# A mixture-of-experts layer on one core: the closing sum split over ScalarE, VectorE and GpSimd, with the first gated rows in PSUM

## What is computed

```python
x = x + attention(layernorm(x))
n = layernorm(x)
route_w = softmax(n @ Wr + br)                  # 8 experts
routed  = route_w * mask_of_the_top_2
routed  = routed / routed.sum(-1)               # two gates for each token
h       = relu(n @ W1[e] + b1[e])               # each expert, 128 -> 512
y[e]    = h @ W2[e] + b2[e]                     # 512 -> 128
out     = x + sum_e routed[e] * y[e]
```

## Time and profile before

| | |
|---|---|
| time before, median of 3 runs | 353.44 us (353.34 to 354.66) |
| the profiled execution: its own time | 355.26 us |
| its span | 353.5 us |
| busy in the span: PE, DVE, ACT, POOL | 294.8, 285.2, 222.9, 249.3 us |
| last scatter issued by GpSimd | 329.50 us |
| first of the eight loads issued | 332.47 us |
| first scaling and first sum | 336.27 and 336.28 us |
| last sum ends | 350.77 us |

### The profile page before, as it was taken

The page is one execution under the profiler, slowest core; times in us unless marked ns, Lnnn a source line. Parts: engine busy times, 40 slices in busy tenths (PEclk is TensorE's granted clock), DMA queues, the critical chain, the costliest instruction groups (busy, mean ns, idle before and its releaser), DMA issues.

```text
span 353.5 us, 7837 instructions
## 1 busy us (share of the span) xinstructions
PE 294.8 (83%) x2237; PEld 209.9 (59%) x2237; DVE 285.2 (81%) x623; ACT 222.9 (63%) x644; POOL 249.3 (71%) x251
## 2 busy tenths in 40 slices
PE   5899999989979999799867699999999999997000
PEld 5677845545545555555424477778888888886000
DVE  5888899999886999999899549997777777772196
ACT  2688711488878745245434886768888888882092
POOL 4639995454979998898777477777777777777300
PEclk9899999999999999899969589999999999997555
DMA  8990000000000000001111266525655454411397
GB/s 227 351 289 19 2 0 0 0 4 0 1 0 0 2 23 26 23 23 53 56 45 52 48 98 109 100 71 96 103 100 107 107 100 108 105 58 52 106 401 236
DMA packets 50026, 29.16 MB, mean 82 GB/s; under 512 B 34993, under 2 KB 44639, under 8 KB 49986
## 3 DMA queue, kind: packets, MB, share of 16 engines
q1 hardware_dynamic: 45142, 19.02, 22.4%
q0 software_dynamic: 4544, 9.38, 9.5%
q10 hardware_dynamic: 300, 0.27, 0.2%
HBM read 10.87 MB, written 12.67 MB: 67 GB/s over the span
## 4 chain that ended last, share of the span: by engine, by line
PE 41%; DVE 29%; issue 10%; ACT 9%; POOL 8%; DMA 2%; POOLq 0%; ACTq 0%; DVEq 0%; SPq 0%
PE ps L1260 9%; POOL y_rows L554 7%; PE ps L1259 5%; DVE nd L914 4%; DVE work L903 4%; PE ps L1233 3%; PE ps L1421 3%; PE ps L1423 2%; PE ps L1422 2%; DVE rows L930 2%; PE ps L1440 2%; PE ps L1441 2%; PE ps L1445 2%; DVE x L1194 2%; DVE wraw L1145 2%
## 5 line engine op out<-in xcount | busy, mean ns | idle before, releaser
L554 POOL DMA_INDIRECT y_rows<-kvt,yid x78 | 74.7, 958 | 23.8 <-issue 21.3
L520 POOL DMA_INDIRECT x_rows<-rows,pos_i x64 | 62.4, 975 | 21.7 <-issue 17.8
L722 ACT ACTIVATE ps<-ps,b1s 128x256 f32<-128x256 f32 x156 | 60.4, 451 | 16.3 <-PE ps L1423 14.1
L1145 DVE TENSOR_TENSOR wraw<-ps,wraw 128x1024 f16<-128x1024 f32 x39 | 47.7, 1224 | 21.1 <-ACT wraw L728 20.8
L1421 PE MATMUL ps<-wraw,w1h 128*128 128x256 f16 x156 | 43.3, 278 | 0.8 <-issue 0.6
L1423 PE MATMUL ps<-wraw,w1l 128*128 128x256 f16 x156 | 43.1, 276 | 0.0
L1422 PE MATMUL ps<-wraw,w1h 128*128 128x256 f16 x156 | 43.1, 276 | 0.0
L914 DVE TENSOR_REDUCE nd<-work 128x144 f32<-128x1152 f32 x32 | 41.8, 1346 | 0.4
L1440 PE MATMUL ps<-w,wraw 128*128 x312 | 40.4, 221 | 0.0
L1441 PE MATMUL ps<-w,wraw 128*128 x312 | 40.4, 222 | 0.0
L903 DVE TENSOR_TENSOR work<-ps,qk 128x1024 f32<-128x1024 f32 x32 | 37.9, 1214 | 2.2 <-PE ps L1260 2.2
(11 more groups left out here) (243 smaller groups left out, 741.0 us busy)
## 6 DMA issues: line engine op xcount, KB each, us to landing
qk<-y_rows SPq DMA_DIRECT2D x8, 512.0 KB, 6.5
wraw<-in_L_ffn_W_dram SPq DMA_DIRECT2D x1, 2048.0 KB, 11.1
out_dram<-x SPq DMA_DIRECT2D x8, 256.0 KB, 4.2
x<-in_L_attn_x_dram SPq DMA_DIRECT2D x3, 512.0 KB, 7.0
y_rows<-kvt,yid POOLq DMA_INDIRECT x78, 2.4
x_rows<-empty SPq DMA_DIRECT2D x9, 130.0 KB, 3.4
x_rows<-rows,pos_i POOLq DMA_INDIRECT x64, 2.3
wraw<-x_rows SPq DMA_TRANSPOSE x39
```

The source lines that it names most:

```text
L520: nc.gpsimd.indirect_dma_start(out=x_rows, out_offset=bass.IndirectOffsetOnAxis(ap=pos_i[:, c, t:t + 1], axis=0), in_=rows[:, t, :], in_of ...
L554: nc.gpsimd.indirect_dma_start(out=y_rows, in_=ysb[:, n % YG, g], in_offset=None, out_offset=bass.IndirectOffsetOnAxis(ap=yid[:, n, g:g + ...
L722: ins = nc.scalar.activation(o, o, ACT.Relu, bias=b1s[:, bass.ds(e * HC + c, 1)])
L1145: nc.vector.tensor_tensor(hl[:, n % HB], inner(n), hh[:, n % HB], ALU.subtract).then_inc(lo_done, 1)
```

## The change

ScalarE's product goes to PSUM, group g to bank g, in place of back into `yg`. VectorE's `scalar_tensor_tensor` reads it from there: yg[:, t, 1] = yg[:, t, 1] * gate2 + first. It doesn't touch x any more, and it waits for ScalarE's four products ahead of its own four, not behind them. The sum with x is one `tensor_tensor` over four tiles: on GpSimd for the groups 0 to 6, after VectorE's four (`mix_half`), and on VectorE for group 7, after everything else that it does. The stores of the groups 0 to 6 wait for GpSimd (`pool_mixed`), the last one for VectorE (`mix_done`).

```diff
+        pool_mixed = sem("pool_mixed")
@@ SyncE
             for g in range(Y_LOADS):
                 gt = slice(g * TPY, (g + 1) * TPY)
-                sp.wait_ge(mix_done, g + 1)
+                if g < Y_LOADS - 1:
+                    sp.wait_ge(pool_mixed, g + 1)
+                else:
+                    sp.wait_ge(mix_done, 1)
                 sp.dma_start(ov[:, gt, :], x[:, gt, :]).then_inc(out_done, 16)
@@ GpSimd
             for n in range(EARLY_Y, NBLK):
                 scatter_y(n)
 
+            for g in range(Y_LOADS - 1):
+                gt = slice(g * TPY, (g + 1) * TPY)
+                pool.wait_ge(mix_half, gt.stop)
+                nc.gpsimd.tensor_tensor(x[:, gt], x[:, gt], yg[:, gt, 1], ALU.add).then_inc(pool_mixed, 1)
@@ ScalarE
             for t in range(NT):
                 act.wait_ge(y_in[t // TPY], 16)
-                nc.scalar.activation(yg[:, t, 0], yg[:, t, 0], ACT.Copy, scale=r1[:, 2, t:t + 1]).then_inc(first_done, 1)
+                nc.scalar.activation(ps[:, t // TPY, t % TPY * D:(t % TPY + 1) * D], yg[:, t, 0], ACT.Copy,
+                                     scale=r1[:, 2, t:t + 1]).then_inc(first_done, 1)
@@ VectorE
             def mix(g):
-                gt = slice(g * TPY, (g + 1) * TPY)
                 dve.wait_ge(y_in[g], 16)
-                for t in range(gt.start, gt.stop):
-                    nc.vector.scalar_tensor_tensor(out=x[:, t], in0=yg[:, t, 1], scalar=r1[:, 7, t:t + 1], in1=x[:, t],
+                dve.wait_ge(first_done, (g + 1) * TPY)
+                for t in range(g * TPY, (g + 1) * TPY):
+                    first = ps[:, g, t % TPY * D:(t % TPY + 1) * D]
+                    nc.vector.scalar_tensor_tensor(out=yg[:, t, 1], in0=yg[:, t, 1], scalar=r1[:, 7, t:t + 1], in1=first,
                                                    op0=ALU.mult, op1=ALU.add).then_inc(mix_half, 1)
-                dve.wait_ge(mix_half, gt.stop)
-                dve.wait_ge(first_done, gt.stop)
-                nc.vector.tensor_tensor(x[:, gt], x[:, gt], yg[:, gt, 0], ALU.add).then_inc(mix_done, 1)
 
             for g in range(Y_LOADS):
                 mix(g)
+            last = slice(NT - TPY, NT)
+            dve.wait_ge(mix_half, NT)
+            nc.vector.tensor_tensor(x[:, last], yg[:, last, 1], x[:, last], ALU.add).then_inc(mix_done, 1)
```

## The result

The changed kernel takes 358.19 us (median of 9 runs, 356.63 to 359.03) where the kernel before, beside it, takes 354.67 (353.34 to 355.75). The ratio is 1.009, with a 95% interval of 1.0063 to 1.0117. The profiled execution has a span of 356.7 us instead of 353.5. The forecast was 351.7 us, from a kernel before at 353.44, which is a ratio of 0.995.

The account below looks back on a forecast made before the run. VectorE's chain of sums was taken to bound the last stage; relieved of it, the queue of stores would, the last landing at 351.35 us for 353.1. So 353.44 - 1.75 = 351.7 us, range 351.1 to 352.8.

Parts of the forecast that it names:

- What bounds the kernel: Opening step, last stage: VectorE is the chain, its last sum ending at 350.77 us, the last store landing at 353.1.
- 0.4 us of ending: End of the kernel: time added after the last store lands at 353.1 us, making the span 353.5.
- It is the only thing on GpSimd's queue there: Last stage: GpSimd's sums with x have its queue to themselves, the last scatter being at 329.5 us.
- the 1.75 of the forecast: Last store: landing at 351.35 us in place of 353.1, so 1.75 us less.
- VectorE's four sums: Last stage, per group: four `scalar_tensor_tensor` stay at 1.14 us with one input from PSUM.
- The 0.26 us more: VectorE's four sums: extra cost estimated from the skill's 120 fixed cycles for a PSUM source against 58 for SBUF.
- ScalarE to PSUM: ScalarE's scalings in the last stage: between 0.26 and 0.33 us for one written to PSUM, 0.32 taken.
- GpSimd's sum: Sum with x, groups 0 to 6: 1.2 us each with hand-over, bounds 1.1 to 1.45, keeping up with VectorE.
- The last sum of VectorE: Group 7's `tensor_tensor` with two SBUF inputs, at 347.8 us: a wait of 0 to 0.5 us for GpSimd.
- The lock: Shared SBUF way: VectorE with two SBUF inputs contends with GpSimd, 4796 ns for 422; with at most one it does not.
- the lock holds here too: Rival, last stage: the gate read from SBUF makes VectorE and GpSimd take turns, about 358 us; chance 0.06.
- The stores as the floor: Last stage: from 346.1 us stores land every 0.75 us, the eighth at 351.35, hiding up to 0.45 us in the sums.

Follow-up runs that it names:

- e10: Changed kernel with a GpSimd drain behind its last scatter, but ScalarE's products left in SBUF, in place; ratio 1.0081 to the kernel before.
- e7: Changed kernel with one more drain on GpSimd's queue, between its last scatter and its first sum; ratio 0.9954 to the kernel before.
- e8: Kernel before with a GpSimd drain behind its last scatter, then a wait for VectorE's eighth group; ratio 0.9982.
- e11: Same kernel as e7, measured again; ratio 0.997 to the kernel before.
- e4: Kernel before with only a wait for VectorE's eighth group added to GpSimd's queue, no work; ratio 1.0176.
- e12: Kernel before with seven more GpSimd drains, behind its 1st, 3rd, 7th, 15th, 31st, 63rd and 111th indirect DMA; one execution, drain lengths read, no ratio given.

## Why the prediction was wrong

**What bounds the kernel** was the step that failed. I took "0.4 us of ending" behind the last store as a constant and never asked which engine arrives last at the end of the block. The busy times and the timeline leave the drains out: they aren't counted as work, and GpSimd looks empty after 330.5. One view that I did read names the closing drain, the chain of work before the change, though not its length:

```profile
327.93 1.26 POOLq L91
```

The rows of line 91 had the answer: a drain on GpSimd of 11.5 us that ended at 339.0 with 14 us to spare.

**"It is the only thing on GpSimd's queue there"** is the same fault at the place of the edit. The closing drain stood behind the new sums, and they moved it from 339.0 to 356.4. I asked what the moved work passes and who waits for it, but not what stands behind it. The term was missing from the sum, and it is nearly the whole error. From the last store's landing to the end of the span it was 0.4 us before and is 5.3 after, 4.8 us more; the forecast of the span, 351.75, was 4.9 too low.

The rest is two things that nearly cancel. The last store landed at 351.4 and before at 353.1, 1.7 us earlier, which looks like the 1.75 of the forecast, but by luck: 0.6 us is that the stage began earlier in this execution. The stage itself won 1.1 us. Its eighth load landed 13.5 us behind the first issue, not 12.8 as before, and the stores began to land at 346.1 in both.

**The rest of the sum held.** VectorE's four sums: 1.14 forecast, 1.12 measured, one input from PSUM costing nothing (343 ns in median, 344 before). The 0.26 us more by the figures of the Trainium skill (VectorE: DVE Perf Modes, section on the TRN2 errata) are not to be seen. ScalarE to PSUM: 0.32 us forecast for one, 7.67 / 24 = 0.32 measured. GpSimd's sum: 1.2 forecast, 1.26 measured; it kept pace with the groups. The last sum of VectorE, which reads two tensors of SBUF, was not held (0.69 us), but it started at 347.94, just when GpSimd's last ended, so this run doesn't say what an overlap would have cost. The lock: e10 shows that it is real and that PSUM avoids it; the rival "the lock holds here too" is out, since the gate read from SBUF doesn't bring it on. The stores as the floor: from 346.1 they landed every 0.76 us up to the last, which took 2.8 us to land and not 2.3, as forecast (the forecast's own sum, 346.1 + 7 * 0.754, is 351.38 and not 351.35).

With the drain out of the way, the forecast can be read off e7. From the first load's issue to the end of the span the kernel before takes 21.0 us (20.9 in e8, on e7's chip). e7 takes 19.3, 1.7 to 1.8 us less with 1.75 forecast, and e11 takes 19.5, 1.5 less. As ratios, 0.9954 and 0.997 for a forecast of 0.995. The eighth load lands 12.7 us behind the first issue in e7 and 13.0 in e11, so how fast the loads come decides part of the gain.

**The rivals and the range.** The range ended at 352.8, and 0.06 was given to the side above 355, by a mechanism that didn't happen. Among the rivals was none in which an engine is late for the end without anything waiting for its result.

## What to carry to other kernels

Before work is given to an idle engine at the end of a kernel, look at what stands behind it on that engine's queue, the closing drain included, and at the slack of each engine at the final barrier. When a wait at the end of the block names an engine that has long been done, list the drains of that line. On GpSimd with indirect DMAs behind it, put a drain where the engine is idle anyway: in this kernel it turned a ratio of 1.006 to 1.009 into 0.995 to 0.997.

## What the runs showed of the hardware

- GpSimd's drain takes 8.5 us behind 142 indirect DMAs, 20 us after the last of them as well as at once (e4, before), 43 ns when another drain has been there since (e8), and 1.4 us behind a single one (e12). In e4 the DMAs had landed long before: SyncE's loads, which wait for the last scatter, were issued at 332.2, and the drain ran from 350.6 to 359.1.
- A `scalar_tensor_tensor` on VectorE with two tensors from SBUF stands still while GpSimd runs a `tensor_tensor` (e10, up to 1422 ns for 340); with one tensor from PSUM and its scalar from SBUF it does not (340 to 348 ns over 32, beside GpSimd's seven).
- ScalarE's row of 128 columns is 36 ns shorter into PSUM than into SBUF (356 for 392 ns on average), but the next one starts no sooner: 0.32 us from one start to the next in both kernels.
